# Keys and values first: reordering the loads, maxima and scales at the start of a cross-attention and mixture-of-experts kernel

## The reference

```python
def _L0_xattn_ref(q, latent_kv, Wq, Wkv_expand, Wout):
    qp = q @ Wq.T
    kv = latent_kv @ Wkv_expand.T
    k, v = jnp.split(kv, 2, axis=-1)
    ...
    scores = jnp.einsum('bhqd,bhkd->bhqk', qh, kh) * inv_sqrt_d
    ...
    attn = jax.nn.softmax(scores, axis=-1)
    out = jnp.einsum('bhqk,bhkd->bhqd', attn, vh)
    ...
    return out @ Wout.T

x = x + _L0_xattn_ref(_layernorm(x), ctx_512, Wq, Wkv_expand, Wout)
x = x + _L0_ffn_ref(_layernorm(x), router_w, wg, wu, wd, sg_w, sg_b, su_w, su_b, sd_w, sd_b)
```

## Time and profile before

| | us |
|---|---|
| median of 3 runs | 790.71 (790.65 to 793.01) |
| time of the profiled execution | 791.66 |
| its span, from first to last instruction | 789.9 |
| PE busy | 760.1 |
| DVE busy | 579.8 |
| ACT busy | 460.0 |
| POOL busy | 433.8 |

### The profile page before, as it was taken

One profiled execution on the slowest core, in us unless ns is written; L12 is line 12 of the kernel. 1 busy time (PEld: TensorE's weight loads), 2 busy tenths in 40 slices (PEclk: granted clock), 3 DMA queues, 4 the chain that ended last, 5 costly groups with the idle time before them and its releaser, 6 DMA issues.

```text
span 789.9 us, 21975 instructions
## 1 busy us (share of the span) xinstructions
PE 760.1 (96%) x7252; PEld 520.8 (66%) x7252; DVE 579.8 (73%) x1199; ACT 460.0 (58%) x847; POOL 433.8 (55%) x563
## 2 busy tenths in 40 slices
PE   5898999999999999999999999999999999999995
PEld 2767888888888887778888864455554545455552
DVE  5999999999989898856898765555555555565552
ACT  4688888998898989775556333333333333333330
POOL 2455787777777777552200203756565565656543
PEclk9999999999999999999999999999999999999998
DMA  8326867777676777778666646989898888979992
GB/s 293 125 78 182 230 192 223 214 211 212 197 217 200 217 220 215 202 221 264 209 201 202 227 137 124 163 136 161 140 156 140 149 144 152 147 134 163 145 148 34
DMA packets 138319, 140.73 MB, mean 178 GB/s; under 512 B 87872, under 2 KB 88896, under 8 KB 137856
## 3 DMA queue, kind: packets, MB, share of 16 engines
q1 hardware_dynamic: 122336, 104.01, 48.6%
q0 software_dynamic: 15904, 35.70, 26.0%
HBM read 71.61 MB, written 52.31 MB: 157 GB/s over the span
## 4 chain that ended last, share of the span: by engine, by line
PE 84%; DVE 7%; DMA 5%; issue 2%; ACT 1%; POOL 0%; SPq 0%; DVEq 0%; POOLq 0%; ACTq 0%
PE psum L1456 45%; PE psum L1525 19%; PE psum L1447 10%; PE psum L1575 5%; DMA hidT<-xn2p 4%; PE psum L1618 3%; DVE kv_store L974 1%; DMA out<-w_q,tabs 1%; DVE head_max L1162 1%; DVE stats L1078 1%; PE psum L1504 1%; DVE probsT L974 1%; DVE w_q L1436 0%; DVE attnT L1132 0%; DVE xn1T L974 0%
## 5 line engine op out<-in xcount | busy, mean ns | idle before, releaser
L732 POOL DMA_INDIRECT out<-w_q,tabs x71 | 112.5, 1584 | 110.7 <-DVE w_q L1436 80.5
L722 POOL DMA_INDIRECT x_in<-normed_tokens,tabs x71 | 71.4, 1006 | 89.9 <-DVE tabs L1315 42.2
L925 ACT ACTIVATE silu_g<-psum,tabs 128x256 f32<-128x256 f32 x71 | 33.6, 473 | 146.0 <-PE psum L1456 143.9
L1421 DVE SCALAR_TENSOR_TENSOR hid<-psum,tabs,silu_g 128x256 f32<-128x256 f32 x71 | 34.3, 484 | 111.2 <-ACT silu_g L925 108.1
L1456 PE MATMUL psum<-exp_all,hidT 128*128 x426 | 103.4, 379 | 3.2 <-DMA hidT<-xn2p 3.2
L1456 PE MATMUL psum<-exp_all,probsT 128*128 x420 | 96.4, 379 | 0.0
L1525 PE MATMUL psum<-xn1T,w_q 128*128 128x128 f16 x1536 | 91.0, 219 | 0.8 <-DVE maxima L957 0.8
L1456 PE MATMUL psum<-w_o,attnT 128*128 128x512 f16 x384 | 88.0, 379 | 1.7 <-DVE attnT L1132 1.3
L1525 PEld LDWEIGHTS psum<-xn1T,w_q 128*128 128x128 f16 x1536 | 86.3, 98 | 2.1 <-issue 2.1
L574 POOL TENSOR_TENSOR exp_all<-piece,exp_all 128x512 f32 (+1 forms) x48 | 56.0, 1166 | 44.5 <-ACT piece L752 44.5
L1456 PEld LDWEIGHTS psum<-exp_all,hidT 128*128 128x128 f16 x426 | 41.7, 98 | 54.2 <-issue 6.2
(11 more groups left out here) (216 smaller groups left out, 1652.0 us busy)
## 6 DMA issues: line engine op xcount, KB each, us to landing
x_in<-x SPq DMA_DIRECT2D x64, 256.0 KB, 3.1
exp_all<-experts SPq DMA_DIRECT2D x24, 512.0 KB, 5.2
out<-xy SPq DMA_DIRECT2D x32, 256.0 KB, 3.2
normed_tokens<-xn SPq DMA_DIRECT2D x32, 256.0 KB, 5.2
normed_turned<-xn2T SPq DMA_DIRECT2D x32, 256.0 KB, 3.4
w_q<-out SPq DMA_DIRECT2D x32, 256.0 KB, 2.9
out<-w_q SPq DMA_DIRECT2D x32, 256.0 KB, 2.1
probsT<-normed_turned SPq DMA_DIRECT2D x16, 256.0 KB, 3.5
```

The lines of the kernel that those rows point to most:

```text
L722: pool.indirect_dma_start(x_in[:, t % 4, :], None, xn_dram, bass.IndirectOffsetOnAxis(gather_at[:, t:t + 1], 0)).then_inc(gathered[t % 4], 16)
L732: pool.indirect_dma_start(out, bass.IndirectOffsetOnAxis(add_at[:, t:t + 1], 0), y[:, t % Y_RING, :], None, bounds_check=TOKENS - 1, oob_i ...
L925: act.activation(silu_g[:, :], psum[:, GU_BANK[m % 2], 0:I], ACT.Silu, scale=gate_scale_at[:, tm:tm + 1]).then_inc(silu_ready, 1)
L1421: dve.scalar_tensor_tensor(hid[:, :], psum[:, GU_BANK[m % 2], I:2 * I], up_scale_at[:, tm:tm + 1], silu_g[:, :], ALU.mult, ALU.mult).then_ ...
```

## The change

It renames the groups, so that group 1 is the context, w_k and w_v and group 2 is w_q alone, and puts everything of the old second group ahead of everything of w_q.

- SP loads w_k, the context twice and w_v ahead of w_q, directly behind tile 0.
- PE makes the first key product ahead of turning tile 0, the second behind it, then turns group 1, makes the third key product, spreads group 1 and makes the fourth. Then follows w_q's group, turned and spread, then the first values and the q product. Turning group 3 (w_o and router) moves behind the first q product and its spreading behind turning tile 1.
- DVE takes the three maxima and all scales of keys and values first, then w_q's maximum, its scale, and both low halves one behind the other. `largest(3)` moves behind the low parts of keys and first values.
- ACT writes the high part of the keys ahead of w_q's halves, that of the first values behind them, and the sums of w_o and router last.
- In the step of tile 5, DVE reads the spread maxima of group 4 ahead of the softmax's subtraction instead of behind it.

No work is added or removed. In the diff the first `first_weights` is ACT's, the second DVE's.

```diff
-M_WQ, M_CTX, M_WK, M_WV, M_WO, M_R, M_GU, M_DOWN, M_BIAS = range(9)
+M_CTX, M_WK, M_WV, M_WQ, M_WO, M_R, M_GU, M_DOWN, M_BIAS = range(9)
 N_MAG = 9
-GROUPS = ((M_WQ, M_CTX), (M_CTX, M_WO), (M_WO, M_GU), (M_GU, N_MAG))
+GROUPS = ((M_CTX, M_WQ), (M_WQ, M_WO), (M_WO, M_GU), (M_GU, N_MAG))
 MAGS = M_WO
-MAG_BANK = (5, 4, 4, 5)
+MAG_BANK = (4, 5, 4, 5)
...
             load_x(0, 0)
-            sp.dma_start(wq_raw, wqT).then_inc(wq_in, 16)
             sp.dma_start(wk_sb, wkT).then_inc(ctx_in, 16)
             for d in range(2):
                 sp.dma_start(ctx_sb[:, :, d, :], ctxT).then_inc(ctx_in, 16)
             sp.dma_start(wv_sb, wvT).then_inc(ctx_in, 16)
+            sp.dma_start(wq_raw, wqT).then_inc(wq_in, 16)
...
             def first_weights():
+                act.wait_ge(k_mm, 1)
+                act.wait_ge(scales_ready, 1)
+                copy(k_all[:, 0, :, :].rearrange("p c k -> p (c k)"), bank(0, 4), sc[:, S_K:S_K + 1], k_hi)
                 act.wait_ge(wq_scale_ready, 1)
                 for half in range(2):
                     here = slice(half * C * H // 2, (half + 1) * C * H // 2)
                     copy(w_q[:, 0, here], wq_raw[:, here], sc[:, S_TMP:S_TMP + 1], wq_hi)
+                high_values(0)
                 act.wait_ge(wo_in, 32)
                 row_sums(M_WO, wo_raw)
                 act.wait_ge(sums_ready, 1)
                 row_sums(M_R, r_raw)
-                act.wait_ge(k_mm, 1)
-                act.wait_ge(scales_ready, 1)
-                copy(k_all[:, 0, :, :].rearrange("p c k -> p (c k)"), bank(0, 4), sc[:, S_K:S_K + 1], k_hi)
-                high_values(0)
...
             def first_weights():
-                dve.wait_ge(wq_in, 16)
-                magnitude(M_WQ, wq_raw)
-                turn_first(0)
-                largest(1)
-                spread_maxima(1)
-                powers(1)
-                dve.tensor_scalar(col(sc, S_TMP), col(inv2, M_WQ), W_UP, None, ALU.mult).then_inc(wq_scale_ready, 1)
                 dve.wait_ge(ctx_in, 64)
                 magnitude(M_CTX, staged[0])
                 magnitude(M_WK, wk_sb)
                 magnitude(M_WV, wv_sb)
+                turn_first(0)
+                largest(1)
+                context_scales()
+                dve.wait_ge(wq_in, 16)
+                magnitude(M_WQ, wq_raw)
+                largest(2)
+                spread_maxima(2)
+                powers(2)
+                dve.tensor_scalar(col(sc, S_TMP), col(inv2, M_WQ), W_UP, None, ALU.mult).then_inc(wq_scale_ready, 1)
+                link(dve.tensor_scalar(col(sc, S_EXP), col(sc, S_EXP), col(pow2, M_WQ), None, ALU.mult))
                 dve.wait_ge(wq_scale_ready, 1)
-                largest(2)
                 query_low(0)
-                context_scales()
                 query_low(1)
...
             def first_splits():
-                largest(3)
                 dve.wait_ge(k_hi, 1)
                 low(k_all[:, 1, :, :].rearrange("p c k -> p (c k)"), bank(0, 4), col(sc, S_K),
                     k_all[:, 0, :, :].rearrange("p c k -> p (c k)"), k_split)
                 low_values(0)
+                largest(3)
...
             def first_products():
-                turn_magnitudes(1)
-                spread_magnitudes(1)
                 pe.wait_ge(ctx_in, 4 * 16)
                 for c in range(C):
+                    if c == 1:
+                        turn_first(0)
                     if c == 2:
-                        turn_magnitudes(2)
+                        turn_magnitudes(1)
                     if c == 3:
-                        spread_magnitudes(2)
+                        spread_magnitudes(1)
                     last = pe.matmul(psum[:, c, :].rearrange("p (b k) -> p b k", b=B), wk_sb[:, c * P:(c + 1) * P],
                                      ctx_sb[:, :, 0, :], start=True, stop=True)
                 last.then_inc(k_mm, 1)
+                turn_magnitudes(2)
+                spread_magnitudes(2)
                 pe.wait_ge(xn1T_ready, 1)
                 values(0)
-                turn_magnitudes(3)
...
                 if isinstance(t2, int) and t2 == 0:
-                    spread_magnitudes(3)
+                    turn_magnitudes(3)
...
                 if live(t1) and not (isinstance(t1, int) and t1 == 0):
                     turn_first(t1)
                 if isinstance(t2, int) and t2 == 0:
+                    spread_magnitudes(3)
                     pe.wait_ge(k_split, 1)
                     values(1)
...
                 if scaled is not None:
                     expert_scales(scaled, 4)
+                if isinstance(b, int) and (b, j) == (1, 1):
+                    spread_maxima(4)
                 if live(t2):
                     dve.wait_ge(max_ready, t2 + 1)
                     dve.tensor_tensor(probs[:, :, :], scores, head_max[:, :, None].to_broadcast([P, NH, SK]),
                                       ALU.subtract).then_inc(shifted, 1)
-                if isinstance(b, int) and (b, j) == (1, 1):
-                    spread_maxima(4)
```

More of the change, by code:

```diff
@@ L1000, in context_scales @@
             def context_scales():
-                spread_maxima(2)
-                powers(2)
+                spread_maxima(1)
+                powers(1)
                 link(dve.tensor_scalar(col(sc, S_K), col(inv2, M_WK), col(inv2, M_CTX), KV_UP, ALU.mult, ALU.mult))
@@ L1009, in context_scales @@
                                        ALU.mult, ALU.mult))
-                link(dve.tensor_scalar(col(sc, S_EXP), col(sc, S_EXP), col(pow2, M_WQ), None, ALU.mult))
             def late_scales():
@@ L1472, in turn_magnitudes @@
                 if group != 3:
-                    pe.wait_ge(mags_ready, (1, 4, None, 5)[group - 1])
+                    pe.wait_ge(mags_ready, (3, 4, None, 5)[group - 1])
                 if group == 3:
```

## The result

| | before | changed |
|---|---|---|
| median, 10 runs each | 791.12 us | 795.39 us |
| lowest to highest | 788.46 to 793.92 | 794.33 to 798.16 |
| ratio to before, 95% interval | | 1.0054, 1.0035 to 1.0072 |
| profiled execution, its span | 791.66, 789.9 | 794.61, 792.9 |

The changed kernel is slower by 4.3 us, with an interval of 2.8 to 5.7 (0.0035 and 0.0072 of 791). Ratios leave out slow executions, those over 1.5% above the fastest of their kernel; only the changed kernel with the warm-up has any, two of eleven, and one of them is its profiled one.

The account below looks back on a forecast made before the run. PE is busy for 96% of the span, but at the start it waits for DVE. Terms of 4.0 + 0.3 + 0.4 - 0.4 give +4.3 us, a median of 795.0, range 792.1 to 797.4.

Parts of the forecast that it names:

- the prediction's own sign: Wrong in size if one of the listed start times in the changed profile is off by more than 0.5 us.
- Landing: Start, loads: the context group takes w_q's place and has landed at 7.4 us, bounds 6.4 and 7.8.
- PE up to the first spreading: Start, PE from 7.45 us: three key products, turnings and spreading take 6.45 us, so the spread maxima are there at 13.9.
- Context scales, w_q's maximum, w_q's scale, halves: Start, behind the first spreading: 1.2, 2.29 and 2.4 us, then w_q's halves; q product at 23.7 against 19.72, +4.0 us.
- Order of group 3: Before the first scores: group 3's spreading ahead of the values adds a turn on PE, +0.3 us, bounds 0 and 0.4.
- Clock at the q product: First q product: PE idles some 4 us before it, so it may run at half clock; +0.4 us, bounds 0 and 1.7.
- The first rival: Start: half clock throughout, in the third key product and the q product; +6.0 us or 796.7; 20%.
- Group 4: Step of tile 5: PE's 0.79 us wait before a q product goes; -0.4 us, bounds 0 and -0.75.
- The second: Start and tile 5: delay mostly taken up, group landing at 6.4, products at full clock; +1.8 us, 792.5; 16%.
- The third: Start: DVE runs through without waiting, w_q split at 17.3, deciding point before 17.6; faster, -2.7 us, 788.0; 5%.

Follow-up runs that it names:

- the changed kernel with the warm-up: The changed kernel with 22 turnings of the identity matrix on PE before the loads come: 1.0098 of before; the same on the kernel before: 1.0046.
- the version with one chain: The changed kernel with w_q loaded first, the context loaded once and one chain for all four weights: median 788.12 us, 0.9972 of before.

## Why the prediction was right

The forecast was +4.3 us for a slower kernel; +4.3 was measured. The direction and the mechanism hold: the chain of the context group in front of w_q's puts the q product 4.07 us later where 4.0 was forecast. The agreement to a tenth is luck. The pair of profiles is only 2.95 us apart (794.61, where 796.0 was forecast), the interval is 2.8 to 5.7, and two terms were wrong by more than a microsecond each, in opposite directions. By the prediction's own sign, a row off by more than 0.5 us, it was wrong in size at the landing (8.87 for the first maximum, where 7.4 was forecast).

- *Landing*: 7.4 forecast, 8.8 measured, outside the bounds of 6.4 to 7.8. The time from w_k's landing to w_v's in the trace of before, 3.05 us, was taken for a duration that would stay. In the changed kernel w_v lands 5.2 us behind tile 0 (3.6), where 0.75 + 3.05 = 3.8 was forecast. This term was mis-sized by 1.4. With the context loaded once the group lands at 6.2.
- *PE up to the first spreading*: 6.45 forecast, 14.11 - 8.98 = 5.1 measured. I had the clock rise with the third key product; it rose with the second (1.13 us). That is 1.3 the other way. The two errors cancelled, and line 957 came at 14.14 against 13.9. The clock's rise differs from run to run (1.13, 1.50, 1.76, 1.91 and 1.92 us for this product in five profiles of the changed lists), so this agreement is luck.
- *Context scales, w_q's maximum, w_q's scale, halves*: 1.2, 2.29, 2.4 and 3.85 forecast; 1.2, 2.29, 2.2 and 3.9 measured, the last from ACT's start at 19.87 to 23.79. The q product was forecast for 23.7 and started at 23.79.
- *Order of group 3*: +0.3 forecast, 0.41 measured as the distance from the q product to head_max (9.53 against 9.12). The values start 0.31 later behind the q product, and the run that put group 3 back takes just this 0.31 away. The sum behind it is another than was said: the turning of tile 1 comes 0.45 earlier, since `largest(3)` no longer stands in front of the low parts of keys and values, and the spreading with its wait for DVE's diagonal puts 0.76 in front of the values.
- *Clock at the q product*: +0.4 forecast with a bound of 1.7. In the profile of the changed kernel the product ran at full clock. Where it ran partly at half clock, 4.35 us, head_max followed after the same 9.5 us. The term should have been near 0 in such a case, and the price in the rival was too high. The 4 us of idleness that it was built on were not there either: PE waited 2.54 us ahead of w_q's turning, and the values stood at 19.01 to 22.5, so only 1.27 us were left before the q product. What costs is half clock one step later, at the values behind the turning of tile 1, which I had not priced: DVE then waits 1.9 to 2.2 us for the scores instead of 0.3 to 0.5. It was so in six of the fourteen profiles, in lists of both orders, though not in the two that the prediction compares.
- *Group 4*: -0.4 forecast, -0.50 by the rows, and for the reason given: DVE's attention is next.

The first rival, half clock throughout, came true in part, at the first values, where it is hidden. The second fails: the group landed late, not early, and up to 60 us nothing was taken up on the way, though of its terms the third key product and the q product did run at full clock. The third needed w_q split before 17.6; it was split at 23.6. Its idea was not wrong, only its place: in the version with one chain w_q is split at 16.7.

The reason that was argued, one chain in front of the other, is shown best by one run: w_q's maximum moved alone brings the q product back by 2.1 us. The one chain with the context loaded once brings it to 18.14, ahead of 19.72 before, but that kernel differs in its loads too; with the context loaded twice the one chain has it at 21.08, still 2.7 us ahead of the changed kernel. Open is how much of the measured 4.3 us comes from the additional half clock in most executions of the changed kernel.

## What to carry to other kernels

Two chains that cross several engines cost little as long as each fills the other's waits; here, to put one wholly in front of the other made the q product 4.07 us late without a single instruction of work added. When reordering a start, ask of every input what waits between its landing and its first use: w_q lay ready for 3.9 us. And do not judge a start by one profile: in five profiles of the changed lists the same key product took 1.13 to 1.92 us, and in fourteen profiles the values behind tile 1 took 1.88 to 3.66, by the clock. Nor should the profile of the start be taken for the whole: with the warm-up the start was faster and the kernel slower.

## What was not expected of the hardware

- The granted clock is shown as 1.00 from the start of the span, while PE's first records run at half pace (four in 3.78 us, the same four in 1.98 after 22 turnings); later falls it does show, as 0.50.
- With the context in runs of 256 bytes, loaded twice, the group lands at 8.8 us; its two issues hold SP for 1.42 us and w_v's behind them for 1.10 (3.05 in the kernel before). Once, in rows of 2 KB, the group lands at 6.2 and each issue takes 0.42 or 0.43.
- In ten profiles PE waited 1.57 or 1.82 us in front of the turning of tile 1. In five of them the value products behind it ran at half clock (3.10 to 3.66 us), in the other five at full clock (1.88 or 1.98).
- Bringing the clock up before the loads land shortens the start by 1.6 us in the profiled execution and lengthens the median by 3.6 us. In the one profile that shows a loss, that of the changed kernel with the warm-up, it lies in the second phase, in longer waits for DMA transfers and half clock behind two of them; why is not known.
